# Recommendation tower: another layout of the broadcast ids, signals per table, and another order of ScalarE's first work

## What is computed

```python
e = jnp.stack([tbl_f[ids[:, f]] for f in range(27)], axis=1)
dot = jnp.einsum('bnd,bmd->bnm', e, e)          # the pairs below the diagonal
h = jnp.concatenate([z, dense_ctx], axis=1)
h = jnp.maximum(h @ W_top1 + b_top1, 0.0)
h = jnp.maximum(h @ W_top2 + b_top2, 0.0)
y = h @ W_top3
```

## Time and profile before

| | |
|---|---|
| median of 3 runs | 410.06 us (409.57 to 411.84) |
| profiled execution, its own time | 410.82 us |
| its span, first to last instruction | 409.0 us |
| TensorE busy (matmul) | 340.1 us, 83% |
| VectorE busy | 276.8 us, 68% |
| ScalarE busy | 153.9 us, 38% |
| GpSimd busy | 264.1 us, 65% |
| mean granted TensorE clock | 0.958 |
| moved by DMA | 35.77 MB, 87 GB/s |

### The profile page before, as it was taken

The page is one execution under the profiler, slowest core; times in us unless marked ns, Lnnn a source line. Parts: engine busy times, 40 slices in busy tenths (PEclk is TensorE's granted clock), DMA queues, the critical chain, the costliest instruction groups (busy, mean ns, idle before and its releaser), DMA issues.

```text
span 409.0 us, 15028 instructions
## 1 busy us (share of the span) xinstructions
PE 340.1 (83%) x6064; PEld 297.6 (73%) x6064; DVE 276.8 (68%) x733; ACT 153.9 (38%) x212; POOL 264.1 (65%) x281
## 2 busy tenths in 40 slices
PE   0094824599989998999999999999998999899876
PEld 0093824499867896789768986888778976898665
DVE  2295761959855996689776986599669966881240
ACT  0637822212442335323443244324422353324432
POOL 5777757775377757776777767776677777771000
PEclk9999695679999999999999999999999999999899
DMA  4879964261632633241526453242415282210000
GB/s 132 221 195 250 197 118 104 55 109 46 76 79 60 100 69 100 58 105 47 127 53 67 96 76 98 66 91 73 108 46 104 63 116 53 60 53 21 3 6 0
DMA packets 29867, 35.77 MB, mean 87 GB/s; under 512 B 12921, under 2 KB 23809, under 8 KB 29842
## 3 DMA queue, kind: packets, MB, share of 16 engines
q1 hardware_dynamic: 21010, 17.32, 24.5%
q0 software_dynamic: 8832, 18.11, 16.3%
HBM read 35.39 MB, written 0.01 MB: 87 GB/s over the span
## 4 chain that ended last, share of the span: by engine, by line
PE 65%; ACT 10%; DVE 9%; issue 9%; DMA 4%; SPq 1%; ACTq 0%; DVEq 0%
PE emb_ps L622 28%; PE gram_ps L654 12%; PE mlp_ps L675 10%; DVE onehot L514 9%; PE mlp_ps L689 7%; ACT embT L402 5%; PE emb_ps L645 3%; DMA turned<-in_tbl 2%; DMA ids_b<-in_ids_mm 2%; ACT onehot L390 2%; PE mlp_ps L697 1%; ACT parts L381 1%; PE mlp_ps L718 1%; PE mlp_ps L723 1%; ACT onehot L393 1%
## 5 line engine op out<-in xcount | busy, mean ns | idle before, releaser
L359 POOL DMA_INDIRECT rows<-in_tbl,idx x272 | 259.0, 952 | 104.7 <-DMA rows<-in_tbl,idx 75.0
L514 DVE TENSOR_SCALAR onehot<-ids_b,row_of 128x256 fp32r<-128x256 int32 x608 | 188.1, 384 | 22.2 <-PE emb_ps L622 15.3
L622 PE MATMUL emb_ps<-onehot,parts 125*128 125x256 f32 x1248 | 164.2, 292 | 37.3 <-ACT parts L381 25.8
L622 PEld LDWEIGHTS emb_ps<-onehot,parts 125*128 125x128 f32 x1248 | 157.2, 196 | 40.6 <-ACT parts L381 27.0
L398 ACT ACTIVATE embT<-emb_ps 128x512 f32<-128x512 f32 x40 | 48.1, 1220 | 112.2 <-PE emb_ps L622 112.2
L654 PEld LDWEIGHTS gram_ps<-embT 128*32 128x32 f32 x4096 | 45.3, 113 | 40.7 <-issue 38.5
L654 PE MATMUL gram_ps<-embT 128*32 128x26 f32 x4096 | 53.6, 197 | 19.1 <-issue 16.0
L520 DVE COPY embT<-emb_ps 128x512 f32<-128x512 f32 (+1 forms) x32 | 31.5, 1054 | 42.0 <-PE emb_ps L645 42.0
L645 PE MATMUL emb_ps<-ident,rows 128*128 128x128 f32 x272 | 40.6, 294 | 8.3 <-ACT embT L402 7.5
L402 ACT ACTIVATE embT<-emb_ps 128x512 f32<-128x512 f32 (+1 forms) x48 | 44.6, 1074 | 1.3 <-PE emb_ps L645 1.1
L413 ACT ACTIVATE h<-mlp_ps,b_sb 128x256 f32<-128x256 f32 x42 | 17.6, 470 | 69.7 <-PE mlp_ps L689 31.1
(11 more groups left out here) (37 smaller groups left out, 96.3 us busy)
## 6 DMA issues: line engine op xcount, KB each, us to landing
ids_b<-in_ids_mm SPq DMA_DIRECT2D x8, 768.0 KB
rows<-in_tbl,idx POOLq DMA_INDIRECT x272, 2.5
ids_b<-in_ids_mm SPq DMA_DIRECT2D x16, 256.0 KB, 6.0
turned<-in_tbl SPq DMA_DIRECT2D x6, 448.0 KB
h<-in_tbl SPq DMA_DIRECT2D x2, 448.0 KB
blocks<-in_tbl SPq DMA_DIRECT2D x2, 448.0 KB
w_sb<-in_W_top SPq DMA_DIRECT2D x1, 512.0 KB, 7.7
w_sb<-in_W_top SPq DMA_DIRECT2D x2, 224.0 KB
```

The source lines that it names most:

```text
L359: pool.indirect_dma_start(rows[:, t, n, :], None, tables[f], bass.IndirectOffsetOnAxis(idx[:, t, f:f + 1], 0), engine_sem=gathers_written) ...
L514: last = nc.vector.tensor_scalar(onehot[:, k % OH, c, :], ids_b[:, k, :], row_of[:, c:c + 1], None, ALU.is_equal)
L622: last = nc.tensor.matmul(emb_ps[BANK[k]][:, m * W:(m + 1) * W], parts[0:MP, f, part, c * D:(c + 1) * D], onehot[0:MP, f % OH, c, :], star ...
```

## The change

Three things are edited. The ids lie in DRAM as [8 pairs, 10 tables x 256 samples], and `load_ids` reads, for each partition, one run of 2 KB or 6 KB. A lookup has a signal for each of its tables: `s_looked` is raised after the first table and `emb_filled` after the second; VectorE and ScalarE wait for a mask slot on the signal of the table that held it (`slot_free`), and TensorE waits for each table's mask on its own. In the head ScalarE copies tables 0 to 2 ahead of the mask of table 3.

```diff
+        s_looked = sem("s_looked")
...
+        def looked(p, k):
+
+            if isinstance(p, int) and p == 0:
+                return k + 1
+            return p * LOOK + k
+
+        def slot_free(eng, p, f):
+
+            if f % LOOK_TABLES:
+                eng.wait_ge(emb_filled, p * JOBS + f // LOOK_TABLES + 1)
+            else:
+                eng.wait_ge(s_looked, looked(p, f // LOOK_TABLES))
...
                 a, b = IDS[h].start, IDS[h].stop
-                src = ids_mm[a:b, bass.ts(p, W)]
-                sp.dma_start(ids_b[:, a:b, :], src.partition_broadcast(P)).then_inc(s_ids[h], 16)
+                src = ids_mm[bass.ds(p, 1), a * W:b * W].rearrange("one n -> (one n)")
+                sp.dma_start(ids_b[:, a:b, :].rearrange("p f w -> p (f w)"), src.partition_broadcast(P)
+                             ).then_inc(s_ids[h], 16)
...
                 if f >= OH:
-                    act.wait_ge(emb_filled, (f - OH) // LOOK_TABLES + 1)
+                    slot_free(act, 0, f - OH)
...
-            make_onehot(ACT_ONEHOTS[0])
             for k in range(NM):
-                if k == ACT_ONEHOTS[1]:
+                if k in ACT_ONEHOTS[:2]:
                     make_onehot(k)
                 split_high(k)
...
                 dve.wait_ge(s_ids[ids_part(k)], (p + 1) * 16)
-
                 if k >= OH:
-                    dve.wait_ge(emb_filled, p * JOBS + (k - OH) // LOOK_TABLES + 1)
-                else:
-                    held = max(f for f in range(NM) if f % OH == k)
-                    past(dve, emb_filled, (p - 1) * JOBS + held // LOOK_TABLES + 1)
+                    slot_free(dve, p, k - OH)
+                elif not (isinstance(p, int) and p == 0):
+                    held = [f for f in range(NM) if f % OH == k and not (isinstance(p, int) and p == 1 and f in EARLY)]
+                    slot_free(dve, p - 1, held[-1])
...
                 bank_free(p, k)
-                if not (isinstance(p, int) and p == 0):
-
-                    pe.wait_ge(s_onehot, BUILT + (p - 1) * NM + max(OH, (k + 1) * LOOK_TABLES))
                 for m in range(LOOK_TABLES):
...
+                    else:
+
+                        pe.wait_ge(s_onehot, BUILT + (p - 1) * NM + max(OH, f + 1))
...
-                last.then_inc(emb_filled, 1)
+                    last.then_inc(emb_filled if m else s_looked, 1)
...
-    ids_mm = give("in_ids_mm", ids_in[:, MM_TABLES].T)
+    ids_mm = give("in_ids_mm", ids_in[:, MM_TABLES].reshape(PAIRS, W, NM).transpose(0, 2, 1).reshape(PAIRS, NM * W))
```

## The result

| | before | after |
|---|---|---|
| median, 4 runs each in one comparison | 410.01 us (409.57 to 411.84) | 384.01 us (383.83 to 385.45) |
| profiled execution, its own time | 410.82 us | 383.83 us |
| its span | 409.0 us | 382.0 us |

The ratio is 0.937, with an interval of 0.934 to 0.940.

What follows compares the result with a forecast made beforehand. TensorE's work plus a mask wait bounds each pair; the slow ids broadcast delays the head. 14.0 + 5.8 + 0.8 = 20.6 us off 410.8 gives 390.2, as median 389.5 us; range 386 to 404.

Steps and rivals of the forecast that it cites:

- step 3: Lookups of pairs 1 to 7: a signal per table removes TensorE's mask wait, 5.8 us plus 0.8 in pair 1.
- step 1: Head: contiguous ids speed the broadcast, so table 4 and Gram of tile 1 come sooner; 14.0 us, ends 16.1 and 10.8.
- Step 2: Head: ScalarE splitting tables 0 to 2 first starts TensorE sooner, but table 4's landing covers it; 0 us.
- GpSimd under the pair: Loop: GpSimd's 42.4 us of gathers stay 0.4 us under the 42.8 us pair, close but no wait.
- A: Ids load: the broadcast gets no faster, the head stays and only the signals gain; 403.4 us, chance 0.25.
- B: Head: the broadcast is fast but TensorE's Gram hole has another cause, head gains 6.7 us; 396.7 us, chance 0.20.
- C: Head ids load: one run per partition makes the broadcast slower than 73 GB/s; 425 us at half rate, chance 0.05.
- D: Pairs: VectorE's order takes the signals' gain back and the broadcast is no faster; 409 to 410 us, chance 0.03.

Runs made afterwards that it cites:

- f3: The kernel before with the new layout of the ids alone: 395.24 us, ratio 0.962 to the kernel before.
- e3: The kernel before with ScalarE's new order alone, in a comparison where the kernel before took 721.71 us: 719.49 us, ratio 0.996.
- e11: The kernel before with ScalarE's new order alone, repeated where the kernel before took 723.38 us: 723.48 us, ratio 0.999.
- f2: The changed kernel with ScalarE's old order, so layout and signals only: 385.05 us, ratio 0.939 to the kernel before.
- e7: The kernel before, with SP loading pair 1's third ids part only after tile 0's Gram products: 405.64 us, ratio 0.995.
- g1: The kernel before with ids by pair, table, sample, in 1 KB pieces 2304 bytes apart where it was 8192: 395.38 us, ratio 0.963.

## Why the prediction fell short

**The sum.** 20.6 us were forecast and 27.0 came between the profiled executions. Of the 6.4 that are missing, 3.0 lie ahead of pair 1 (14.0 forecast, 17.0 measured), 2.0 in pair 1 (0.8 and 2.8) and 1.5 in the six pairs and the tail after it (5.8 and 7.3). By parts, step 3, the signals, was the most mis-sized; in step 1 it was the landing of the last gather.

**The bound.** Right. One pair was TensorE's work plus the wait for masks, and the head was late by the broadcast. After, the mask wait is gone from the pairs and TensorE is busy for 89% of the span.

**Step 1, layout: 14.0 forecast, 15.0 measured (f3).** The mechanism and its chain came as told. Table 4: 25.0 forecast, 25.3 in f3 and 23.9 with all three parts. The hole: 4.3 forecast, 1.03 and 0.74; it was worked out as 10.96 less 6.7, what the broadcast for pair 0 was to save. The one beside the hole saved more: from its issue to its last bytes it took about 12.2 us before (52.8 to 65.0) and 4.0 in f3 (45.7 to 49.8), and Gram's first part ran for 3.18 us in place of 1.85 before it stopped. It cost nothing, because the last gather is what comes next, as the step says. That gather landed at 51.74 + 2.53 = 54.3, where 57 was chosen out of 55.0 to 60.3. The longer time in that choice, 7.8 us, was of gathers earlier in the head, and those are nearly as slow in the changed kernel (its gathers in 0 to 60 us whose landing the trace tells):

```profile
DMA to landing us min/median/max: 5.0/7.0/7.7
```

The last gather is another case: from 50 to 56 us SP's queue moves 0.01 MB. The middle between the two medians was the wrong choice. Gram of tile 1 followed at 55.85 in the changed kernel (58.6 forecast), 2.7 us sooner, and at 57.56 in f3, where VectorE's move came last. The layout alone brings pair 1 forward by 15.3 us (81.06 - 65.73), 1.3 more than forecast; the other 1.6 of the 17.0 came with the other two parts.

**Step 2, order: 0 forecast, 1.8 measured, not told from 0.** Its cover was named as table 4's landing. In the kernel before that holds (e3 and e11, seen only where it takes 720 us). With the fast broadcast the cover is another, the gathers: the order brings Gram of tile 0 forward by 3 us (47.01 to 44.06), and pair 1 by 0.4. Two details were off: TensorE starts at 9.94, not at 16.1, since table 0 had landed long before ScalarE's wait for ids ended, and SP then issues table 4 at 12.9 rather than at 17.

**Step 3, signals: 6.6 forecast, 10.2 measured (f3 to f2).** This is the step that failed, by its size. The price per pair was read from the idle time of TensorE's matmuls, 0.96 us. The rows of its weight loads in the same pair of the kernel before, which the prediction did not use, say 1.17:

```profile
225.15 3.85 PEld L622 LDWEIGHTS emb_ps<-onehot,parts 125*128 125x128 f32 x32 [1.17 <-DVE onehot L514]
```

and 1.2 is what a pair gained (43.8 to 42.6). Ahead of the stop the last weight load ends at 223.98 and the last matmul at 224.18, and the end of a matmul in the profile is modelled. Six pairs make 7.0 in place of 5.8. In pair 1 the 0.8 became 2.7 (its length is 47.06 in f3 and 44.35 in f2): its wait went (0.93 in f3), the first, slow lookup took 5.54 us in place of 6.48, and the rest are shorter waits; the step had held these fixed. Between the profiled executions of f3 and f2, whose spans are 393.8 and 381.9 us, the 11.9 us are 1.0 in the head (65.73 to 64.77), 2.7 in pair 1, 5.5 in pairs 2 to 6, and 2.7 in pair 7 and the tail. Pairs 2 to 5 gained 1.2 to 1.4 each, and pair 6 only 0.3, for a wait of 1.95 us for ScalarE's move stands in it. In pair 7 the wait for the mask went (1.08); what else differs there is not settled, as two late stops of TensorE vary from run to run, one between 1.8 and 2.5 us and one between 0.9 and 1.8.

**GpSimd under the pair.** Its slack was put at 0.4 us per pair, "close, but no wait". In the middle pairs TensorE waits for no rows, as told; GpSimd's gathers, one each 1.25 us, take 42.4 of the 42.6 us, and its only long waits there are the two of 1.6 us. In the head and pair 1 it is a bound, as the step said it would be if the head gained more than forecast: the 17.0 us gained stand against 14.0, and TensorE waits 3.1 us for rows.

**The rivals.** A (the broadcast no faster, 403.4) is refuted by 3.6 against 6.0 us. B (a hole of another origin, 396.7) by e7. C did not come; one run per partition is as fast as the pieces of g1. D is refuted by the pair of 42.6. The range was drawn towards A and B, and below by the ends of step 1 alone; step 3 was given no range, though its 0.96 us came from a single row whose end is modelled.

## What to carry to other kernels

When a load seems slow, look at what it keeps waiting besides its own reader: here the pieces of a broadcast that lay 8 KB apart moved 73 GB/s, and table loads, gathers and instructions stood behind it; packing what one load reads closely together took 15 us off, for a line of host layout. An idle time with no semaphore to blame can be looked up in the DMA queues: whether an instruction packet moves when it ends. Where a wait is to be removed, read its length from the weight loads as well as from the matmuls, and give it a range. Where two engines finish a head within a microsecond of each other, an edit to one of them shows nothing; try both before either is called worthless.

## What was not expected of the hardware

- The rate of the broadcast goes by where its pieces lie and hardly by their size: 1 KB pieces 8192 bytes apart 73 GB/s, 8448 apart 105, 1280 apart 232, 2304 apart 255; runs of 6 KB 255.
- While the slow broadcast ran, no instruction packet moved and the gathers' queue all but stood (0.27 MB in 11.5 us, then 0.39 MB in 2.4).
- In two of the five comparisons each kernel took about 720 us, with matmuls issued singly, 1 to 2.4 us apart, and the record gives one of them the chip on which the kernel before took 410 us in another. What sets this off was not found.
- ScalarE's function table is loaded at 0.82 when a copy is its first work in the program, and at 13.76 when a mask that waits for ids is the earlier trace rows. In the kernel before it came behind the wait for the ids, in the changed one ahead of the wait for table 0, and so it costs nothing there.
- The granted clock in the changed kernel, from the busy times by stretch (us, PE, PEld, DVE, ACT, POOL busy, clock, DMA share, GB/s):

```profile
44.00:56.00 12.00, 6.76 (x284) 5.72 (x288) 8.98 (x22) 4.04 (x5) 9.02 (x10) 0.79 0.30 87
56.00:64.00 8.00, 5.13 (x259) 4.46 (x256) 6.49 (x19) 1.32 (x2) 6.09 (x7) 0.50 0.22 57
```

  From 56 to 64 us it stands at 0.50, the lower of the two levels, after a stretch of Gram products with stops; the first lookup of pair 1 takes 5.81 us, where the same 32 matmuls take 4.02 in a middle pair.
